# Adding the last four pairs' expert rows to tiles 0 and 1 by 0/1 matrix products

## The chip, the cores and the metric

The kernel runs on one core of one Trainium2 chip. The metric is the device time of one execution in microseconds. TensorE (PE) multiplies matrices, VectorE (DVE) and ScalarE (ACT) work element by element, GpSimd (POOL) does so too and issues indirect transfers, and SyncE (SP) issues the plain transfers. The five engines run their own instruction queues in order and wait for each other by semaphores.

## What is computed

Two layers on 2048 tokens of width 256. The part that matters here is the mixture of experts in the first layer and how its result is used:

```python
topk_w, topk_idx = jax.lax.top_k(scores, K)          # K = 8 of E = 64 experts, CAP = 64 slots each
buf  = zeros.at[dest].set(xf[slot_token])            # gather of tokens to expert slots
hmid = silu(einsum(xb, w_gate)) * einsum(xb, w_up)
yb   = einsum("ecf,efh->ech", hmid, w_down)
out  = zeros((T, h)).at[slot_token].add(yb[dest] * topk_w)   # each token adds up its (at most 8) expert rows
...
x  = x + s * silu(out)                               # s: the first layer's spectral mixing
xn = layernorm(x)                                    # the second layer begins: projections, window attention
```

## The kernel before, in words

Tokens are cut into 16 tiles of 128; four tiles are a sequence. The 64 experts are worked as 32 pairs, 128 slots at a time. The kernel has stages, and each ends with a barrier: an engine reports the end of its part to the semaphore `stage` and waits until all five have.

Stage 3 is the pair loop. For pair j, POOL gathers the 128 token rows (`gather_rows`), TensorE turns them, multiplies by the gate and up weights, turns the product (`expert_turn`) and multiplies by the down weights (`expert_down`); VectorE copies the result to `y0[:, j % 4]`. POOL then scatters it (`scatter_rows`, L2331) to the table `z_d` in HBM. `z_d` was cleared before and has for every tile 8 planes of 128 rows: plane k holds the k-th expert row of each token. The row numbers `put0` are worked out by VectorE at the end of the index chain (L1819 to L1835). `keep_clock` (L971) is a pair of matrix products without use, in each pair. Beside the pairs, "units" of the second layer's weights get their low-rank parts added and are split into two f16 halves; 30 of the 32 pairs or so carry one or two. SP writes the units of `wqk` to HBM in four writes of 1 MB (L783), each when its units are done (`lo_done`).

At the end POOL waits for the landing of all scatters and only then reports the stage's end. Behind the barrier SP reads the 8 planes of tiles 1, 0, 3 and 2, 1 MB each (`load_rows`, L789), then weight group 0 and tables. Tiles 0 and 2 are added up by VectorE in three additions (`summed`, L1895 to L1899), tiles 1 and 3 by TensorE as products with the identity (`rows_summed`, L1054). ScalarE takes a tanh of each sum (`half_gate`, L1457), VectorE makes the new x and its statistics (`finish`, L1905 to L1913), and after two tiles their moments (`spreads`). ScalarE normalises (L1468, L1470), TensorE turns the rows (L1062) and ranks the experts of layer two (L1069), and `project(0)` (L1094) begins the attention. The order of VectorE is written out: summed(0), finish(0), finish(1), spreads, summed(2), finish(3), scales, finish(2), spreads. The rows of tiles 4 to 15 are read in halves later (L792), and POOL adds the second halves by accumulating transfers (L2366, L2371) between its sines (L2354).

## Time and profile before

| | |
|---|---|
| three timed runs | 1118.9, 1122.3, 1123.69 us (median 1122.3) |
| the profiled execution's own time | 1118.6 us |
| its span, first to last instruction | 1116.6 us |
| busy: TensorE, VectorE, ScalarE, POOL | 89%, 76%, 60%, 49% |
| mean granted TensorE clock | 0.955 |

Times in a trace count from the start of the span. The pair loop lies between about 128 and 235 us, and the first projection of the second layer starts at 271.87. A pause of an engine costs time only if the chain that ends last runs through it.

### The profile page before, as it was taken

Reading aid. Unit: us, or ns where it says so; the run is one execution under the profiler, and the core shown is the slowest. Engines: PE = TensorE matmul, PEld = TensorE weight load, DVE = VectorE, ACT = ScalarE, POOL = GpSimd, SP = SyncE. Lnnn points to the kernel's source line nnn. Section 1 sums busy time; section 2 is a strip of 40 time slices with the busy share of each in tenths; the row PEclk is TensorE's granted clock in tenths of the full one; section 3 lists DMA queues with packets and bytes.
Section 4 is the critical chain, followed back from the end, with each engine's and each line's share of the span. In section 5 each row is a group of like instructions: output and inputs, shape, how many; then the busy total and the mean of one; then the engine's idle time right before and its main releaser. Section 6 shows DMA issues by size and latency. Waiting matters only on the chain.

```text
span 1116.6 us, 22230 instructions
## 1 busy us (share of the span) xinstructions
PE 988.5 (89%) x6749; PEld 650.3 (58%) x6749; DVE 851.8 (76%) x2241; ACT 667.4 (60%) x1739; POOL 544.5 (49%) x538
## 2 busy tenths in 40 slices
PE   3967879856999999999999999999988899999985
PEld 2535533334565676666666766767654678885443
DVE  4787548846798779768668899999856887775777
ACT  1733425524768766977866666666646877775332
POOL 0489556621755565544444444544521345553774
PEclk9987989976999999999999999999999999999997
DMA  9979699879562466121211001210049345553443
GB/s 340 338 220 368 161 261 289 287 259 279 81 166 76 115 117 144 36 74 39 63 53 39 32 8 39 91 39 1 1 135 322 98 134 145 147 139 92 133 131 95
DMA packets 97023, 155.99 MB, mean 140 GB/s; under 512 B 12272, under 2 KB 67312, under 8 KB 94096
## 3 DMA queue, kind: packets, MB, share of 16 engines
q1 hardware_dynamic: 77184, 115.42, 31.5%
q0 software_dynamic: 19728, 39.21, 15.8%
q8 instruction: 56, 0.92, 0.3%
q14 instruction: 55, 0.45, 0.1%
HBM read 104.84 MB, written 45.02 MB: 134 GB/s over the span
## 4 chain that ended last, share of the span: by engine, by line
PE 56%; DVE 14%; ACT 9%; issue 6%; DMA 4%; POOL 4%; DVEq 4%; POOLq 1%; ACTq 1%; SPq 0%
PE ps L1094 9%; PE ps L1266 6%; PE ps L1158 5%; PE ps L1146 5%; PE ps L1108 5%; PE ps L1126 3%; PE ps L1212 3%; PE ps L1229 3%; ACT arena L1522 2%; PE ps L1284 2%; PE ps L991 1%; PE ps L1136 1%; PE ps L1008 1%; PE ps L1256 1%; DVE x_sb L1909 1%
## 5 line engine op out<-in xcount | busy, mean ns | idle before, releaser
L2354 POOL TENSOR_TENSOR arena<-arena 128x512 f32<-128x512 f32 x128 | 174.6, 1421 | 98.3 <-ACT arena L1499 98.2
L1094 PE MATMUL ps<-arena 128*128 128x512 f16 x768 | 178.4, 383 | 1.3 <-ACT arena L1499 1.3
L2359 POOL TENSOR_TENSOR arena<-arena 128x512 f32<-128x512 f32 x64 | 67.7, 1057 | 176.0 <-DVE arena L2003 176.0
L2396 POOL DMA_INDIRECT wvo<-xn_d,idx x79 | 75.7, 958 | 113.5 <-PE ps L1256 96.4
L1094 PEld LDWEIGHTS ps<-arena 128*128 128x128 f16 x768 | 75.3, 98 | 93.9 <-ACT arena L1499 3.5
L1522 ACT ACTIVATE arena<-arena 128x128 f32<-128x128 f32 x256 | 99.2, 390 | 38.6 <-DVEq L1998 38.6
L1498 ACT ACTIVATE arena<-ps 64x512 f32<-64x512 f32 x128 | 76.0, 593 | 52.0 <-DVE arena L1971 48.4
L1158 PE MATMUL ps<-wvo,arena 128*128 128x256 f16 x768 | 95.1, 276 | 6.0 <-DVE s_sb L2023 3.2
L1146 PE MATMUL ps<-arena 128*128 128x192 f32 (+1 forms) x512 | 94.5, 328 | 2.4 <-DVE arena L2009 2.4
L1971 DVE TENSOR_TENSOR arena<-ps,wvo 128x512 f32<-128x512 f32 x128 | 84.7, 684 | 15.0 <-PE ps L1094 14.4
L1108 PE MATMUL ps<-wvo,arena 128*128 128x512 f16 x384 | 93.0, 379 | 2.9 <-issue 1.5
L1158 PEld LDWEIGHTS ps<-wvo,arena 128*128 128x128 f16 x768 | 75.4, 99 | 26.0 <-issue 4.3
L1146 PEld LDWEIGHTS ps<-arena 128*128 128x128 f32 x512 | 82.4, 192 | 13.4 <-issue 10.8
L1981 DVE TENSOR_TENSOR arena<-arena 128x512 f32<-128x512 f32 x128 | 85.9, 712 | 3.0 <-POOL arena L2354 3.0
L1266 PE MATMUL ps<-arena,wvo 128*128 x474 | 84.3, 315 | 4.0 <-DVE arena L2200 4.0
L2401 POOL DMA_INDIRECT wvo<-y_d,row x64 | 63.7, 995 | 35.7 <-issue 18.6
L1499 ACT ACTIVATE arena<-ps 64x512 f32<-64x512 f32 x128 | 75.3, 589 | 1.5
L1126 PE MATMUL ps<-arena 128*64 128x128 f32 x1024 | 70.8, 281 | 6.0 <-DVE arena L1981 5.8
L1212 PE MATMUL ps<-arena 128*128 128x512 f16 (+1 forms) x288 | 66.0, 387 | 7.8 <-DVE arena L2189 6.9
L1515 ACT ACTIVATE arena<-ps 128x512 f16<-128x512 f32 x64 | 38.2, 597 | 57.6 <-PE ps L1146 56.9
L1126 PEld LDWEIGHTS ps<-arena 128*64 128x64 f32 x1024 | 55.4, 137 | 16.5 <-issue 15.2
L1995 DVE CUSTOM_DVE_ANT_0 arena<-ps,arena 128x128 f32<-128x128 f32 x256 | 58.6, 284 | 7.0 <-PE ps L1126 6.7
(296 smaller groups left out, 2193.6 us busy)
## 6 DMA issues: line engine op xcount, KB each, us to landing
arena<-wqk_d SPq DMA_DIRECT2D x16, 1024.0 KB, 5.8
arena<-in_wgu SPq DMA_DIRECT2D x32, 384.0 KB, 3.8
y_d<-wvo SPq DMA_DIRECT2D x79, 128.0 KB, 2.4
z_d<-wvo SPq DMA_DIRECT2D x8, 1024.0 KB, 4.3
z_d<-wvo SPq DMA_DIRECT2D x2, 4096.0 KB, 25.6
arena<-in_wdn SPq DMA_DIRECT2D x32, 192.0 KB, 5.3
arena<-z_d SPq DMA_DIRECT2D x12, 512.0 KB, 4.1
arena<-z_d POOLq DMA_DIRECT2D x12, 512.0 KB, 6.7
```

What stands on the lines that cost most here:

```text
L1094: last = pe.matmul(ps[s][:, :], wqk[gg][:, s * DC + c, w, hh * DH:(hh + 1) * DH], hx[bb][:, :, x, c * P:(c + 1) * P], start=(c == 0 and w ...
L1108: last = pe.matmul(values_bank(n, q)[:, :], hx[bb][:, q, x, c * P:(c + 1) * P], wvo16[:, UNITS + c * NG + g, w], start=(c == 0 and w == x) ...
L1126: last = pe.matmul(ps[3][side * WIN:(side + 1) * WIN, q * P:(q + 1) * P], qr[:, u, q * P + side * WIN:q * P + (side + 1) * WIN], kr[:, u, ...
L1146: last = pe.matmul(ps[7][:, k * P:k * P + n], vv[gg][:, k, hh * DH:(hh + 1) * DH], probs[:, k * KW + WIN:k * KW + WIN + n], start=(k == 0) ...
L1158: last = pe.matmul(output_bank(n, half)[:, q % 2 * D:(q % 2 + 1) * D], oT[gg][:, x, hh, q * P:(q + 1) * P], wvo16[:, 2 * g + hh // 2, w, h ...
L1212: last = pe.matmul(ps[2 * (c % 2) + g][0:rows, :], sgw16[:, 2 * d + g, w, c * P:c * P + rows], xb16[:, b % 2, :, x, d * P:(d + 1) * P], st ...
L1266: last = pe.matmul(ps[1 + j % 2][:, 0:2 * F1], xsT[:, j % 4, x, c * P:(c + 1) * P], w13[:, bass.ds(e, 1), w, c * 2 * F1:(c + 1) * 2 * F1]. ...
L1498: nc.scalar.activation(qk_s[0:64, s], ps[s][64:P, :], ACT.Copy)
L1522: nc.scalar.activation(pp[u][:, q], sm[:, q], ACT.Exp, bias=mn[:, q:q + 1], scale=-1.0, accum_out=rs[:, q:q + 1])
L1971: nc.vector.tensor_tensor(qk_c[:, s], ps[s][:, :], cos, ALU.mult).then_inc(cos_rd, 1)
L1981: nc.vector.tensor_tensor(dst, a, b, ALU.add).then_inc(rope_done, 1)
L2354: nc.gpsimd.tensor_tensor(qk_s[:, s], qk_s[:, s], sin, ALU.mult).then_inc(sin_done, 1)
```

## The change

The rows of the last four pairs (28 to 31) that belong to tokens of tiles 0 and 1 are no longer scattered. Their row numbers are raised beyond the table's end, where the scatter's bounds check drops them; the rows of all other tiles are scattered as before. For each of these pairs and each of the two tiles VectorE makes a 128x128 table of zeros and ones early in the pair loop (slot by token: one where the slot holds that token), and TensorE multiplies it with `y0`, which adds the rows into a PSUM bank of the tile. SP reads the planes of tiles 0 and 1 as soon as the scatters of pairs 0 to 27 have landed, inside stage 3, ahead of the last weight write. VectorE adds planes 4 to 7 to planes 0 to 3 (`halved`), and TensorE adds the four that are left into the same PSUM banks. The wait for the scatters' landing moves from POOL, ahead of the barrier, to SP, behind it, ahead of the reads of tiles 3 and 2. Buffers change place so that the early reads find theirs free, and with them the waits of the reads of tiles 4 to 7.

```diff
+        FROM = PAIRS - 4
+        kept_at = {(j, t): R3.take(P, P) for j in range(FROM, PAIRS) for t in range(2) if (j, t) != (PAIRS - 1, 1)}
-        yg_of = [yg[:, 0], yg[:, 1], flat(hx_f[1]...), wqk_f[1]...]
+        yg_of = [wqk_f[1]..., flat(hx_f[1]...), yg[:, 0], yg[:, 1]]
...
-        SUMMED = {0: (mix_done, 1), 2: (mix_done, 2), 1: (table0_mm, 5), 3: (table0_mm, 6)}
+        SUMMED = {0: (table0_mm, 5), 1: (table0_mm, 6), 2: (mix_done, 1), 3: (table0_mm, 7)}
...
-        FIRST_FOUR = (0, 1, 3, 2)
+        FIRST_FOUR = (0, 1, 2, 3)
... SP
+            def put_down(n):
+                for u in range(4):
+                    sp.wait_ge(y0_out[u], 16 * len(range(u, n, 4)))
+            def load_first():
+                put_down(FROM)
+                for t in range(2):
+                    upto(sp, y0_ps, FROM - 1)
+                    load_planes(t)
             for g in range(NG):
+                if g == NG - 1:
+                    load_first()
                 sp.wait_ge(lo_done, 2 * UNITS + 4 * (g + 1))
                 sp.dma_start(wqk_d[g], wqk_parts[:, g]).then_inc(wqk_out, 16)
...
-                    sp.wait_ge(*summed_at(t - TPB))
+                    sp.wait_ge(*summed_at(max(t - TPB, 2 + (t - TPB) // 2)))
...
-            for t in (1, 0, 3, 2):
+            put_down(PAIRS)
+            for t in (3, 2):
                 load_rows(t)
... TensorE
-                keep_clock(6, 2)
+                if j < PAIRS - 1:
+                    keep_clock(6, 2)
...
+            def put_rows(j, t):
+                pe.wait_ge(chosen0, 5)
+                upto(pe, y0_rd, j)
+                pe.matmul(mix_of(t), kept_at[j, t], y0[:, j % 4], start=(j == FROM), stop=False, skip_group_check=True)
...
+                if j >= PAIRS - 2:
+                    for t in range(2):
+                        if j == PAIRS - 2:
+                            put_rows(j - 2, t)
+                        put_rows(j - 1, t)
+            def rows_summed(t):
+                put = t < 2
+                if put:
+                    pe.wait_ge(chosen0, 6 + t)
+                else:
+                    pe.wait_ge(yg_in[t], 16)
+                n = K0 // 2 if put else K0
+                for k in range(n):
+                    last = pe.matmul(mix_of(t), ident[:, :], rows_of(t)[:, k], start=(k == 0 and not put), ...)
+            for t in range(2):
+                put_rows(PAIRS - 1, t)
             stage_end(pe, 3)
...
-            rows_summed(1)
-            rows_summed(3)
+            for t in (0, 1, 3):
+                rows_summed(t)
... VectorE
+            nc.vector.tensor_scalar(rz[:, 0:PAIRS - FROM], tile_no[:, FROM:PAIRS], 2.0, float(NT * K0 * P), ALU.is_lt, ALU.mult)
+            nc.vector.tensor_tensor(row_f[:, FROM:PAIRS], row_f[:, FROM:PAIRS], rz[:, 0:PAIRS - FROM], ALU.add)
+            nc.vector.tensor_copy(rz[:, 0:PAIRS - FROM], idx0[:, FROM:PAIRS])
...
+                if j < 4:
+                    for t in range(2):
+                        nc.vector.tensor_scalar(kept_at[FROM + j, t], iota[:, :], rz[:, j:j + 1], -float(t * P), ALU.subtract, ALU.is_equal)
+                    if j == 3:
+                        dve.drain().then_inc(chosen0, 1)
...
+            def halved(t):
+                a = rows_of(t)
+                dve.wait_ge(yg_in[t], 16)
+                nc.vector.tensor_tensor(a[:, 0:4], a[:, 0:4], a[:, 4:8], ALU.add).then_inc(chosen0, 1)
...
-            summed(0)
+            halved(0)
+            halved(1)
             finish(0)
             finish(1)
             spreads(slice(0, 2))
             summed(2)
+            finish(2)
+            scales(1, slice(0, 2))
             finish(3)
-            scales(1, slice(0, 2))
-            finish(2)
... POOL
-            for u in range(4):
-                pool.wait_ge(y0_out[u], 16 * PAIRS // 4)
             pool.sem_inc(stage, 1)
```

How the instructions stand now is shown at three places. On TensorE at the end of the pair loop, before (L971 is keep_clock, L1000 the turn, L1008 expert_down, L1054 the row sums, a product counted once):

```order
L971 MATMUL ps<-ones_bf 128x512 x2
L1000 MATMUL ps<-ident,arena 96x128
L1008 MATMUL ps<-arena 64x256 x4
L1054 MATMUL ps<-arena,ident 128x256 x16
L1062 MATMUL ps<-ident,arena 128x128 x2
```

and with the change (L1021 is the turn, L1029 expert_down, L1055 the 0/1 products, L1089 the row sums):

```order
L1021 MATMUL ps<-ident,arena 96x128
L1029 MATMUL ps<-arena 64x256 x2
L1055 MATMUL ps<-arena 128x256 x4
L1029 MATMUL ps<-arena 64x256 x2
L1055 MATMUL ps<-arena 128x256 x4
L1089 MATMUL ps<-arena,ident 128x256 x16
L1102 MATMUL ps<-ident,arena 128x128 x2
```

The last keep_clock is gone, four 0/1 products stand between the last two expert_down and four behind them. The number of row sums is the same: four for each of tiles 0 and 1 and eight for tile 3, where it was eight for each of tiles 1 and 3.

On SP from the weight writes on, before (L783 the four weight writes, L789 the planes of tiles 1, 0, 3, 2, L805 group 0):

```order
L783 DMA wqk_d<-arena 128x2048 [waits lo_done] x4
L789 DMA arena<-z_d 128x8x256 [waits stage]
L789 DMA arena<-z_d 128x8x256 x3
L805 DMA arena<-wqk_d 128x2048 [waits wqk_out]
L812 DMA wvo<-in_cos 128x512
```

and with the change (L802 the weight writes, L785 the planes, L824 group 0):

```order
L802 DMA wqk_d<-arena 128x2048 [waits lo_done] x3
L785 DMA arena<-z_d 128x8x256 [waits y0_out3,y0_out2,y0_ps,y0_out1,y0_out0]
L785 DMA arena<-z_d 128x8x256 [waits y0_ps]
L802 DMA wqk_d<-arena 128x2048 [waits lo_done]
L785 DMA arena<-z_d 128x8x256 [waits y0_out2,y0_out1,y0_out3,y0_out0,stage]
L785 DMA arena<-z_d 128x8x256
L824 DMA arena<-wqk_d 128x2048 [waits wqk_out]
```

Two of the four plane reads stand ahead of the last weight write and of the barrier, with waits for scatters of their own.

On VectorE behind the barrier, before (L1895 to L1899 are summed, L1905 to L1913 one finish):

```order
L1895 TENSOR_TENSOR arena<-arena 128x1024 [waits yg_in0,stage]
L1897 TENSOR_TENSOR arena<-arena 128x512
L1899 TENSOR_TENSOR arena<-arena 128x256
L1905 TENSOR_TENSOR arena<-arena,s_sb 128x256 [waits g_ready]
L1907 SCALAR_TENSOR_TENSOR arena<-arena 128x256
```

and with the change (L1939 is halved, L1956 the start of a finish):

```order
L1939 TENSOR_TENSOR arena<-arena 128x1024 [waits yg_in0,stage]
L1939 TENSOR_TENSOR arena<-arena 128x1024 [waits yg_in1]
L1956 TENSOR_TENSOR arena<-ps,s_sb 128x256 [waits g_ready]
L1958 SCALAR_TENSOR_TENSOR arena<-arena 128x256
L1960 TENSOR_TENSOR x_sb<-x_sb,arena 128x256
```

The two small additions of tile 0 are gone, and VectorE now waits for both planes before the first finish, whose input comes from PSUM.

## Rows read from the trace of the kernel before

**Rows 1.** The page: TensorE's busy tenths in 40 equal slices of the span

```profile
PE   3967879856999999999999999999988899999985
```

**Rows 2.** Stretches: length, busy of each engine with its instructions, clock, DMA share, GB/s

```profile
138.00:142.00 4.00, 4.00 (x31) 2.01 (x32) 1.61 (x6) 1.59 (x6) 3.01 (x4) 1.00 1.05 126
...
220.00:230.00 10.00, 10.00 (x70) 4.54 (x70) 8.90 (x20) 5.19 (x14) 3.53 (x5) 1.00 0.81 324
230.00:234.00 4.00, 2.53 (x16) 0.83 (x16) 3.92 (x10) 1.88 (x4) 1.85 (x3) 1.00 0.30 105
...
236.00:238.00 2.00, 0.00 (x0) 0.00 (x0) 0.00 (x0) 0.00 (x0) 0.00 (x0) 0.50 0.98 393
```

**Rows 3.** The chain of waits: start us, us, what

```profile
138.08 12.99 DMA arena<-xn_d,idx
...
234.87 4.04 DMA z_d<-arena,put
...
239.52 8.28 DMA arena<-z_d
```

**Rows 4.** Order in time, 226 to 277: start, us, instructions, idle before

```profile
226.75 0.98 POOL L2331 DMA_INDIRECT z_d<-arena,put  x1 [1.74 <-DVE arena L1879]
...
230.81 0.61 PE L971 MATMUL ps<-ones_bf 128*128 128x512 bf16 x2
...
244.92 5.67 PE L1054 MATMUL ps<-arena,ident 128*128 128x256 f32 x16 [12.39 <-DMA arena<-z_d]
...
250.84 3.72 PE L1054 MATMUL ps<-arena,ident 128*128 128x256 f32 x16 [0.25 <-DMA arena<-z_d]
...
252.79 0.41 DVE L1905 TENSOR_TENSOR arena<-ps,s_sb 128x256 f32<-128x256 f32 x1
...
256.33 1.22 DVE L1895 TENSOR_TENSOR arena<-arena 128x1024 f32<-128x1024 f32 x1
...
258.39 0.43 DVE L1899 TENSOR_TENSOR arena<-arena 128x256 f32<-128x256 f32 x1
...
258.85 0.42 ACT L1457 ACTIVATE arena<-arena 128x256 f32<-128x256 f32 x1 [3.87 <-DVE arena L1899]
...
264.62 0.17 DVE L1924 TENSOR_SCALAR st<-st 128x2 f32<-128x2 f32 x1
...
271.87 4.89 PE L1094 MATMUL ps<-arena 128*128 128x512 f16 x12
```

**Rows 5.** Reads from z_d: L789 all four, its middle two, then L792

```profile
DMA to landing us min/median/max: 5.7/9.5/12.3
...
DMA to landing us min/median/max: 8.3/9.5/10.7
...
DMA to landing us min/median/max: 3.9/4.1/10.2
```

**Rows 6.** Scatters, L2331: the 14 from 200 on, one at 156.8, one at 139.4

```profile
DMA to landing us min/median/max: 2.4/4.3/5.0
...
DMA to landing us min/median/max: 6.7/6.7/6.7
...
DMA to landing us min/median/max: 12.2/12.2/12.2
```

**Rows 7.** Order in time on VectorE, 112 to 137

```profile
112.23 0.68 DVE L680 TENSOR_TENSOR arena<-arena 128x256 f32<-128x256 f32 x1 [3.25 <-ACT arena L1382]
112.84 0.54 DVE L681 TENSOR_TENSOR arena<-arena 128x128 f32<-128x128 f32 x1
...
136.79 0.65 DVE L1864 SCALAR_TENSOR_TENSOR arena<-ps,arena 64x96 f32<-64x96 f32 x2 [0.83 <-ACT arena L1424]
```

**Rows 8.** Order in time on POOL, 260 to 277

```profile
260.18 1.41 POOL L2366 DMA_DIRECT2D arena<-z_d  x1 [24.33 <-DMA arena<-z_d]
...
271.66 1.62 POOL L2366 DMA_DIRECT2D arena<-z_d  x1
...
276.75 1.26 POOL L2354 TENSOR_TENSOR arena<-arena 128x512 f32<-128x512 f32 x1 [3.47 <-ACT arena L1499]
```

More of the change, by code:

```diff
@@ L780, in _, with load_planes @@
                 load_experts(j)
+            def load_planes(t):
+                sp.dma_start(rows_of(t), z_d[t * K0 * P:(t + 1) * K0 * P, :].rearrange("(k p) d -> p k d", p=P)).then_inc(yg_in[t], 16)
+            def put_down(n):
[6 more added lines that the diff above has]
+                    load_planes(t)
             for g in range(NG):
+                if g == NG - 1:
+                    load_first()
                 sp.wait_ge(lo_done, 2 * UNITS + 4 * (g + 1))
@@ L788, in load_rows @@
                 if t < TPB:
-                    sp.dma_start(rows_of(t), z_d[t * K0 * P:(t + 1) * K0 * P, :].rearrange("(k p) d -> p k d", p=P)).then_inc(yg_in[t], 16)
+                    load_planes(t)
                 else:
-                    sp.wait_ge(*summed_at(t - TPB))
+                    sp.wait_ge(*summed_at(max(t - TPB, 2 + (t - TPB) // 2)))
                     sp.dma_start(rows_of(t), z_d[t * K0 * P:t * K0 * P + K0 // 2 * P, :].rearrange("(k p) d -> p k d", p=P)).then_inc(yg_in[t % TPB], 16)
@@ L1046, in _ @@
                     low_rank(n)
-            stage_end(pe, 3)
-            def rows_summed(t):
-                pe.wait_ge(yg_in[t], 16)
-                for k in range(K0):
-                    last = pe.matmul(mix_of(t), ident[:, :], rows_of(t)[:, k], start=(k == 0), stop=(k == K0 - 1))
-                last.then_inc(table0_mm, 1)
+                if j >= PAIRS - 2:
[11 more added lines that the diff above has]
+                for k in range(n):
+                    last = pe.matmul(mix_of(t), ident[:, :], rows_of(t)[:, k], start=(k == 0 and not put), stop=(k == n - 1), skip_group_check=True)
+                last.then_inc(table0_mm, 1)
+            for t in range(2):
+                put_rows(PAIRS - 1, t)
+            stage_end(pe, 3)
             def turn_rows(t, bank):
@@ L1883, in _ @@
                     low_part(n)
-            for n in units_at((PAIRS - 1, "end")):
-                add_low_rank(n)
-                low_part(n - 1)
-                low_part(n)
+                if j < 4:
[3 more added lines that the diff above has]
+                        dve.drain().then_inc(chosen0, 1)
             stage_end(dve, 3)
+            def halved(t):
+                a = rows_of(t)
+                dve.wait_ge(yg_in[t], 16)
+                nc.vector.tensor_tensor(a[:, 0:4], a[:, 0:4], a[:, 4:8], ALU.add).then_inc(chosen0, 1)
             def summed(t):
@@ L1898, in summed @@
                 dve.drain()
-                nc.vector.tensor_tensor(mix[:, u], a[:, 0], a[:, 1], ALU.add).then_inc(mix_done, 1)
+                nc.vector.tensor_tensor(mix[:, 0], a[:, 0], a[:, 1], ALU.add).then_inc(mix_done, 1)
             def finish(t):
```

12 lines of the change are left out of this document (7 added, 5 removed).

## The prediction

> **What bounds the kernel now.** I began with the page's slices: TensorE is busy nine tenths or more in most of them [rows 1], so an edit pays only where TensorE stands still. The stretches around the change [rows 2] and the order in time [rows 4] show such a place: TensorE does nothing for 12.39 us before 244.92, and is granted 0.50 of its clock from 236 on. The chain of waits [rows 3] says why: the last scatter of expert rows (issued 234.87, landed 238.91), the reads of the four token tiles behind it (239.52 to 247.8), VectorE's sums and gates, and only at about 272 the first projection. From there TensorE is busy almost without a gap to the end, so I take what the first projection gains as gained at the end. The order in time then gives the step that ends last for each tile, and the landing times [rows 5, 6] say what a transfer takes, alone and beside others.
>
> Before, the four reads issued at 239.1 to 241.5 land 5.7, 8.3, 10.7 and 12.3 us after their issue [rows 5], that is at 244.8, 247.8, 250.8 and 253.8: 3.0 us per megabyte once they follow each other. Tile 2 has landed at 253.8 but VectorE takes it up only at 256.33, behind the two finishes and the moments of tiles 0 and 1, of which finish(1) and the moments take 3.5 us (252.79 to 256.33) [rows 4]. So VectorE's chain decides: call S the end of the third addition of tile 2 (258.39 + 0.43 = 258.82). From S to the end of the second moments (264.62 + 0.17 = 264.79) are 6.0 us, and 7.1 us more to the first projection at 271.87.
>
> **The reads of tiles 0 and 1.** They now wait for the scatters of pairs 0 to 27 alone. Pair 27's is issued at 226.75 [rows 4]; 4.5 us for its landing (between 4.04 and 5.0, which scatters beside a one megabyte write took, [rows 3, 6]) gives 231.3. SP is free then: its third weight write needs only unit 27, which pair 27 finishes, and the fourth waits for unit 31, four pairs on. With the spacing of [rows 5] the planes land at 231.3 + 5.7 = 237.0 and at 240.0; the scatters of pairs 28 to 31 share the engines with them, at most 4 x 128 KB, about 1.5 us at 350 GB/s if all were moved in that time. Half of that is moved by then, of which I charge 0.4: 240.4.
>
> **The tail of the pair loop.** TensorE's keep_clock pair of pair 31 goes (0.6 us, as the 0.61 us row at 230.81), 16 fp32 instructions of 128x256 come, eight of them ahead of expert_down(31). The same shape took 3.72 us for 16 at full clock, 0.233 us each, and 5.67 us for 16 from half clock upward [rows 4]. Eight are 1.9 us; less 0.6 this moves expert_down(31) by about 1.3 us. VectorE's copy behind it stood in VectorE's queue for some 0.8 us of that, so the scatter starts at about 235.3 in place of 234.87: 0.4 us lost. The other eight end at about 236, beside that scatter's issue, and cost nothing. POOL no longer waits for its landings, so the stage ends at 235.3 + 1.0 = 236.3, before the first plane is there.
>
> **The last scatter and tiles 3 and 2.** The scatter of pair 31 now runs beside the two plane reads and the last weight write. The 14 scatters from 200 on took 2.4 to 5.0 us; the 5.0 is of one issued at 221.4, with the DMA engines at 0.81, the 2.4 of one at 231.9, with them at 0.30. Two early ones took 6.7 and 12.2 us, the latter in a stretch in which the engines were full at 126 GB/s [rows 2, 6]. I take 5.3 us, near the 5.0 us row, since the planes come as whole rows at 350 GB/s as before: it lands at 240.6. The bounds are 4.0 and 12.2. Behind it SP issues tiles 3 and 2. The last weight write (1 MB, 3.0 us behind the planes) ends at 243.4, so tile 3 lands at 246.4 and tile 2 at 249.4. The bytes say the same: 5 MB of reads and writes and 0.4 us of scatters from 231.3 + 2.7.
>
> The Trainium skill (page "DMA: Bandwidth & Descriptors", section on latency and other measured facts) speaks against the edit here: access to HBM takes 0.2 us on average but 2 us at high load, and this makes most of a transfer's fixed cost, so a scatter that was nearly alone gets slower once reads are put beside it. By that figure alone the landing would be 2.4 + 1.8 = 4.2 us, an estimate; the rows show a larger step, 2.4 to 5.0 us. The same page (queues, rings and completion order) has each DMA engine take turns between its queues packet by packet, by which the scatter would not stand behind both planes; the 5.0 us row agrees, the 12.2 us row does not.
>
> **VectorE.** For tiles 0 and 1 it does one addition each of 1.22 us in place of three for tile 0: halved(0) 237.0 to 238.3, halved(1) 240.4 to 241.7. TensorE then adds four planes, 8 instructions, 1.9 us at full clock and 2.8 us at half; tanh takes 0.4. That puts finish(1) at 244.0 to 244.9, and the 3.5 us behind it end at 248.4 at the latest, before 249.4. So what ends last is now the landing of tile 2: S = 249.4 + 2.5 = 251.9, 6.9 us earlier.
> Behind S the order is changed: finish(2), which waits for its tanh (258.85, 0.42 us), now stands ahead of finish(3), whose sum was ready. I charge 0.4 us. The rest of the way to the projection is untouched, 7.1 us, of which 4.89 us for the first 12 matmuls come at half clock [rows 4]; TensorE pauses there as before, so I expect the same clock.
>
> **Edits that should cost nothing, or little.** The three small VectorE instructions added to the index chain (each at most the 0.54 us of the much larger row at 112.84 [rows 7], 1.6 us in all) stand before a 3.25 us wait for ScalarE. The eight comparisons that make the 0/1 tables have the 128x128 shape of that row, so at most 4.3 us in all, 1.1 us in each of pairs 0 to 3, where VectorE waits 0.83 us for the row shown and more for the others. Without that cover they would cost up to 4.3 us; what sticks out of it, and what the index chain may take from POOL, which works beside it, lies between 0 and 1 us: I take 0.1, as pairs 4 on wait for gathers (12.99 us, [rows 3]) anyway. The load of group 0 is issued at about 243.4, when the last weight write has landed, and is there by 253, 12 us before it is needed. Rows of tiles 4 and 5 are asked for at S = 251.9 in place of 250.4 and 250.8, 14 us before the projection in place of 21. POOL's chain there was: a first accumulate at 260.18, a third until 273.28, then a wait of 3.47 us until the first sine at 276.75 [rows 8]. Now tile 4 lands at about 256 (4.1 us after 251.9, [rows 5]), the third issue ends 13.1 us later at 269.1, and the sine is due at 270.5. It is hidden by 1.4 us; I charge 0.1 us for the risk.
>
> **Sum**, against the profiled execution: -6.9 + 0.4 + 0.1 + 0.1 = -6.3 us (the 0.4 us of the later scatter is inside S). That execution took 1118.6 us (its span 1116.6, 2.0 around it); with the change 1112.3. It lies 3.7 us below the median of the three timed runs, 1122.3, so on that scale I forecast 1116.0 us. A measurement of this kernel tells about 0.5%, 5.6 us, from no change: the forecast lies just beyond.
>
> **Rivals.**
> A. The planes slow the last scatters more than the 5.0 us row says. At 6.7 us the scatter lands at 242.0; tile 3 then needs 5.7 us from its issue (247.9) and tile 2 comes at 250.9, S = 253.4: -4.8 us. At 9 us it is -2.5. For it: reads and scatters have never run together at this rate in the trace. Against: 14 scatters beside weight loads and writes took 5.0 at most. Some -3.5 us, 1118.8.
> B. Slower: the same place, but the landing is as between 138 and 146, where a gather took 12.99 us [rows 3] and a scatter 12.2 [rows 6]. The scatter would land at 235.3 + 13.0 = 248.3, tile 2 at 257.0, S = 259.5, 0.7 late, and with the 0.6 of the other edits +1.3 us: 1123.6. It decides from a landing of about 11.8 us on. Against: those engines were full at 126 GB/s, while planes move at 350 (1 MB in 3.0 us).
> C. The gain is given back by POOL: if the accumulates take 2 to 4 us longer because the reads are now packed closer, the first sine and with it the first scores come late, -6.3 + 2.5 = -3.8: 1118.5. For it: only 1.4 us of cover is left. Against: the second wait of POOL (0.78) and VectorE take part of it up.
> D. TensorE pauses less and keeps its clock (2.4 GHz in place of 1.2) until the projection: 4.89 becomes 2.45, 2.4 us more: -8.7, 1113.6. For it: the pause behind the loop shrinks from 12.39 us to about 2. Against: between the row sums and the turned rows it still stands idle for some 5 us, and works in short pieces until the projection.
> E. The change does not do what it says: SP reaches the early reads only at 234, because a scatter of pairs 24 to 27 lands late or the third weight write waits. Planes at 239.7 and 242.7; the fourth write follows and tile 2 comes at 252.1: -3.6, 1118.7.
>
> **How the numbers follow.** Forecast 0.52, A 0.14, B 0.06, C 0.10, D 0.12, E 0.06. The forecast's own range is -4.5 to -8 us. Predicted 1116.0. Over the cases -9.5 to about 0 holds 8 in 10, 1112.8 to 1122.3; the three runs lie up to 3.4 us from their median, of which I add part below and nothing much above: 1110.5 to 1122.5. Faster by over 0.5% needs 5.6 us: D nearly all, three fifths of the forecast and a little for how medians scatter, 0.48. Slower by over 0.5% would need B and more, 0.06. The rest, 0.46, is within.
>
> **What would show it.** The first two z_d reads issued at 231 to 232, landing at 237 and 240; pair 31's scatter issued near 235.3 and landing in 5 to 6 us; TensorE's row sums at 238 and 242; VectorE's first addition of tile 2 waiting for a DMA until about 249.4; 4.89 us at the projection, starting near 265.6; POOL waiting for ScalarE, not for the accumulates, at the first sine. The prediction is wrong if the scatter lands later than 243, if VectorE still comes to tile 2 after it has landed, or if the first projection is early but the end is not.

## The result, and the profile after

The changed kernel takes 1117.34 us (median of 16 runs, 1109.98 to 1120.44), the kernel before 1120.1 us beside it (16 runs, 1116.39 to 1123.69). The ratio is 0.9967, 95% interval [0.9952, 0.9981]: 3.7 us faster, 2.1 to 5.4 (the two medians lie 2.8 us apart). That is a real gain, but inside the 0.5% that I called no change. The profiled execution took 1117.38 us, its span is 1115.2 (before 1118.6 and 1116.6).

The order in time of the changed kernel around the stage's end (start, us, instructions, idle time before):

```profile
224.93 0.98 POOL L2383 DMA_INDIRECT z_d<-arena,put  x1 [1.74 <-DVE arena L1923]
...
229.30 1.01 SPq L785 DMA_DIRECT2D arena<-z_d  x2
229.81 1.99 PE L1055 MATMUL ps<-arena 128*128 128x256 f32 x8
...
232.31 1.99 PE L1055 MATMUL ps<-arena 128*128 128x256 f32 x8
...
233.54 0.34 SPq L802 DMA_DIRECT2D wqk_d<-arena  x1
233.65 0.98 POOL L2383 DMA_INDIRECT z_d<-arena,put  x1 [0.91 <-DVE arena L1923]
...
235.22 1.22 DVE L1939 TENSOR_TENSOR arena<-arena 128x1024 f32<-128x1024 f32 x1 [1.70 <-DMA arena<-z_d]
...
238.70 1.23 DVE L1939 TENSOR_TENSOR arena<-arena 128x1024 f32<-128x1024 f32 x1 [2.26 <-DMA arena<-z_d]
...
240.89 0.99 SPq L785 DMA_DIRECT2D arena<-z_d  x2
...
246.82 5.19 PE L1089 MATMUL ps<-arena,ident 128*128 128x256 f32 x16 [4.85 <-DMA arena<-z_d]
...
249.77 1.23 DVE L1946 TENSOR_TENSOR arena<-arena 128x1024 f32<-128x1024 f32 x1 [3.68 <-DMA arena<-z_d]
...
251.83 0.43 DVE L1950 TENSOR_TENSOR arena<-arena 128x256 f32<-128x256 f32 x1
...
257.35 0.55 DVE L1743 TENSOR_SCALAR st<-st 128x2 f32<-128x2 f32 x1
...
258.75 0.17 DVE L1975 TENSOR_SCALAR st<-st 128x2 f32<-128x2 f32 x1
...
266.00 4.86 PE L1134 MATMUL ps<-arena 128*128 128x512 f16 x12
```

Its chain of waits at the same place (start, us, what), to be held against [rows 3]:

```profile
233.65 7.15 DMA z_d<-arena,put
...
241.31 8.43 DMA arena<-z_d
...
266.11 4.75 PE ps L1134 x12
```

The planes of tiles 0 and 1 are read early and have landed at 235.2 and 238.7. VectorE waits 3.68 us for tile 2's planes, where before it came to them late [rows 4]. The last scatter takes 7.15 us, where it took 4.04 [rows 3].

Absolute times mislead here, since the pair loop itself arrives 1.8 us earlier in this trace (pair 27's scatter at 224.93 against 226.75 [rows 4]). So I measure from that scatter's issue, called P27. (A dash stands where the chain doesn't show the landing.) The table holds distances in us, each the difference of two starts in an order in time: from P27 to pair 31's scatter, to the start of VectorE's second addition of tile 2, and to the first projection; then from one mark to the next: POOL's first and last normalisation in the attention (one for each of 64 heads, L2359 before and L2409 after), the first and ninth gather of the last stage, the span's end. The rows below "other chips" are experiments, told of further down.

| kernel | last scatter | its landing | 2nd addition | projection | to 1st norm. | attention | to 1st gather | to 9th | to end |
|---|---|---|---|---|---|---|---|---|---|
| before | 8.12 | 4.04 | 30.87 | 45.12 | 15.31 | 527.17 | 16.32 | 37.07 | 248.86 |
| changed | 8.72 | 7.15 | 26.14 | 41.07 | 15.28 | 528.60 | 17.41 | 39.07 | 248.84 |
| *other chips* | | | | | | | | | |
| changed_again | 8.64 | 7.22 | 26.17 | 40.73 | 15.57 | 526.83 | 18.93 | 39.55 | 273.57 |
| before_hold | 8.12 | 4.06 | 31.06 | 45.30 | 15.06 | 528.03 | 14.87 | 38.20 | 273.01 |
| after_hold | 8.68 | 7.10 | 26.15 | 40.71 | 15.71 | 527.72 | 14.85 | 36.59 | 272.96 |
| undo_early | 8.63 | 3.99 | 31.45 | 46.02 | 15.06 | 528.23 | 17.42 | 37.50 | 271.04 |
| write_last | 8.72 | 6.02 | 24.86 | 39.40 | 19.55 | 527.49 | 16.22 | 39.66 | 271.92 |
| one_plane | 8.67 | 3.98 | 22.65 | 37.56 | 15.49 | 527.72 | 16.14 | 39.51 | 271.75 |
| write_free | 8.67 | – | 24.71 | 39.25 | 16.31 | 527.74 | 18.93 | 37.73 | 272.60 |
| best | 8.63 | 5.17 | 23.91 | 38.31 | 17.48 | 526.83 | 14.86 | 39.84 | 273.14 |
| best_again | 8.72 | 4.99 | 23.69 | 37.85 | 17.63 | 527.66 | 14.85 | 38.01 | 270.28 |
| entry_hold | 8.72 | 7.12 | 25.82 | 39.76 | 14.94 | 527.89 | 14.86 | 38.01 | 272.26 |
| free_gate | 8.71 | – | 24.99 | 39.54 | 14.89 | 531.54 | 17.42 | 37.14 | 271.53 |
| best_gate | 8.72 | – | 25.94 | 40.48 | 15.96 | 532.43 | 14.86 | 38.39 | 275.20 |

In the first two rows the change gains 45.12 - 41.07 = 4.05 us at the first projection and keeps them to the first normalisation. Behind it the trace of the changed kernel is longer by 1.4 us in the attention, 1.1 on the way to the first gather and 2.0 on the way to the ninth.

### The profile page after: what moved, and what is told of

Read it like the earlier page. It is cut to its first block, busy times and chain, and to the rows that moved or that the text cites. A ratio compares the mean times of both kernels' runs of the same rounds, so it can differ in the third digit from the quotient of the medians.

```text
span 1115.2 us, 22280 instructions
## 1 busy us (share of the span) xinstructions
PE 992.5 (89%) x6763; PEld 652.6 (59%) x6763; DVE 856.1 (77%) x2251; ACT 668.6 (60%) x1739; POOL 544.6 (49%) x538
## 3 DMA queue, kind: packets, MB, share of 16 engines
q0 software_dynamic: 19728, 38.95, 16.1%
## 4 chain that ended last, share of the span: by engine, by line
PE 58%; DVE 14%; ACT 8%; issue 5%; POOL 4%; DMA 4%; DVEq 3%; POOLq 1%; ACTq 1%; SPq 1%
PE ps L1134 9%; PE ps L1306 6%; PE ps L1198 5%; PE ps L1186 5%; PE ps L1148 5%; PE ps L1166 3%; PE ps L1252 3%; PE ps L1269 3%; ACT arena L1562 2%; PE ps L1324 2%; PE ps L926 2%; PE ps L1029 2%; PE ps L1011 2%; PE ps L1176 1%; PE ps L1296 1%
## 5 line engine op out<-in xcount | busy, mean ns | idle before, releaser
L2409 POOL TENSOR_TENSOR arena<-arena 128x512 f32<-128x512 f32 x64 | 67.7, 1058 | 175.8 <-DVE arena L2055 175.8
```

## The experiments

They ran in three series on three other chips, on which the kernel before takes 1152.17, 1152.66 and 1148.13 us (35, 24 and 35 runs), 2.5 to 2.9% more. All ratios are against the kernel before in the same series. No version below is shown to be faster than the changed kernel itself, which stands at 0.9956 in the second series: all their intervals reach that value or lie above it. Theory A: the early reads carry the gain, they slow pair 31's scatter by being beside it, and the rest is given back by TensorE's clock behind the attention. Its rivals: the gain comes from the order of VectorE and the freed barrier; the scatter is slow because of the weight write or the 0/1 products; POOL's accumulates decide.

**Holding the clock at the end of the attention**, with the change and without it.

```diff
                 turn_probs(h)
+                if h == NH - 1:
+                    keep_clock(0, 8)
...
             attend(NH - 1)
+            keep_clock(0, 5)
...
+            upto(pe, xs_lo, 0)
+            keep_clock(4, 10)
             up_proj(0)
```

> The changed kernel with unused 128x512 products at three places where TensorE waits: 8 behind the last turned probabilities, 5 ahead of the last output quarters, 10 ahead of the first up projection of the routed experts. In the changed kernel's trace TensorE's clock is at half from about 816 to 823 and from 850 to 857, before the change only for 2.9 and 2.7 us. Theory 1 (the clock takes the gain back): the half-clock stretches at 816 and 850 are gone or short, and the end comes (6.9 + 7.0)/2 = about 7 us earlier at most, about 5 to 7 us under the changed kernel, near 1111. Theory 2 (transfers of weights or gathered rows of the last stage decide there, the clock is only a bystander): the clock stays up but the end moves by under 1 us.

> The same unused products in the kernel before. Theory 1: its half-clock stretches there are short in the profiled run (2.9 and 2.7 us), so it gains about 1 to 3 us, and the changed kernel with the same products is then faster than this one by about 4.5 us (0.4%), the lead that it has at the end of the attention in the two traces. Theory 2: no gain, and the distance between the two stays as without the products, 0.33% on the median.

Measured: after_hold 1145.17 us (12 runs), ratio 0.9943 [0.9916, 0.997]; before_hold 1149.19 us (12 runs), ratio 0.9988 [0.9952, 1.0024]. The stretches from the last normalisation to the first gather (length, busy time of PE, PEld, DVE, ACT, POOL with instructions, clock, DMA share, GB/s) stand here for five kernels. The kernel before, on the first chip:

```profile
814.40:830.70 16.30, 11.62 (x84) 9.47 (x82) 7.31 (x11) 3.49 (x7) 1.01 (x2) 0.90 0.24 75
```

The changed kernel there:

```profile
809.90:827.30 17.40, 12.72 (x84) 9.98 (x82) 7.29 (x11) 3.51 (x7) 1.02 (x2) 0.80 0.23 71
```

The changed kernel again, on another chip:

```profile
813.50:832.40 18.90, 14.22 (x84) 11.30 (x82) 7.30 (x11) 3.49 (x7) 1.01 (x2) 0.73 0.21 65
```

The changed kernel with the clock held:

```profile
820.90:835.80 14.90, 13.02 (x97) 9.95 (x95) 7.32 (x11) 3.56 (x7) 1.08 (x2) 1.00 0.27 83
```

The kernel before with the clock held:

```profile
824.40:839.30 14.90, 13.02 (x97) 9.92 (x96) 7.30 (x11) 3.56 (x7) 1.05 (x2) 1.00 0.27 84
```

The same 84 products take 11.62, 12.72 or 14.22 us as the granted clock is 0.90, 0.80 or 0.73, and the stretch grows by the same amount. With 13 products without use more it is 14.9 us at clock 1.00, with the change and without: over the table, the six traces with these products show 14.85 to 14.87 and the eight others 16.1 to 18.9. So this loss is the clock's and no wait of the change. Two traces of the same changed kernel differ by 1.5 us here, so how much of it falls on which kernel is chance. The Trainium skill ("TensorE: Matmul & The Clock Gate", part 1) says that the slow clock is the default and activity releases it, and that the number of slow products at one kernel's start varies from run to run; these rows agree, though this stretch lies in the middle of the kernel.

The way from the first to the ninth gather goes with the clock as well: 36.6 us at a granted clock of 1.00 (after_hold), 37.1 to 38.4 in the eight traces at 0.95 or 0.96, 39.1 to 39.8 in the five at 0.91. But here the products don't hold it reliably: best has them and 0.91.

The end did not follow as expected. The changed kernel was to gain 5 to 7 us by the products. after_hold's ratio is 0.13% below that of changed_again, 1.5 us; they ran in different series, and the intervals overlap. before_hold's 1.4 us lies within the noise. What stands is the distance between the two held kernels, 4.0 us on the medians and 5.5 on the means, where 4.5 was expected.

**Reading tiles 0 and 1 behind the barrier again**, with all else as changed.

```diff
             for g in range(NG):
-                if g == NG - 1:
-                    load_first()
...
             put_down(PAIRS)
+            for t in range(2):
+                load_planes(t)
             for t in (3, 2):
                 load_rows(t)
```

> The changed kernel with the reads of tiles 0 and 1 back behind the last scatter's landing (ahead of tiles 3 and 2), all else as changed. Theory A (the early reads carry the gain): the last scatter lands in 4 to 5 us in place of 7.15; the planes land 5.7 to 12.3 us behind it, the first projection comes within 1.5 us of before when counted from pair 27's scatter, and the time is within 0.2% of before. Theory B (the gain is mostly a shorter half-clock stretch at the start of the pair loop, 151 to 154 in place of 150 to 161, and chance): the first projection is still some 2 us earlier than before, with the pair loop earlier by as much, and the time lies between the two kernels.

Measured: 1154.64 us (12 runs), ratio 1.0031 [0.9997, 1.0064]. The chain shows the scatter:

```profile
244.36 3.99 DMA z_d<-arena,put
248.43 5.41 DMA arena<-z_d
```

The projection comes 46.02 us after P27, 0.7 later than in before_hold, the only trace of the old order on these chips. All of the gain at the projection is the early reads'; the 0/1 products, the new order and the freed barrier alone cost a little, as far as one trace of each shows. (The time was to be within 0.2% of before; it is 0.31% above, with an interval from 0.03% below to 0.64% above.) The scatter is back at 3.99 us though the products are there, so these do not slow it.

**What slows the scatter: the last weight write.** The fourth write is moved behind the reads of tiles 3 and 2.

```diff
-            for g in range(NG):
-                if g == NG - 1:
-                    load_first()
-                (wait, write group g)
+            for g in range(NG - 1):
+                keep_group(g)
+            load_first()
...
             for t in (3, 2):
                 load_rows(t)
+            keep_group(NG - 1)
             sp.wait_ge(wqk_out, 16 * NG)
             load_group(0)
```

> The changed kernel with the fourth 1 MB weight write issued behind the reads of tiles 3 and 2, so that pair 31's scatter shares the DMA engines with the two plane reads alone. If the write is half of what slows the scatter (7.15 us from issue to landing, against 4.04 before): landing in 5 to 6 us, tile 2 taken up 1 to 2 us earlier, first projection 1 to 2 us earlier, if VectorE is not the later one. If the planes alone slow it: landing stays near 7 us and nothing moves. Either way group 0 is there 3 us later, unseen.

Measured: 1153.77 us (12 runs), ratio 1.0019 [0.9988, 1.005]. Its chain:

```profile
237.58 6.02 DMA z_d<-arena,put
...
244.73 10.12 DMA wqk_d<-arena
...
257.38 6.16 DMA arena<-z_d
...
264.17 11.14 DMA arena<-z_d
```

and POOL in order of time:

```profile
264.17 1.41 POOL L2419 DMA_DIRECT2D arena<-z_d  x1 [25.60 <-DMA arena<-z_d]
275.60 0.91 POOL L2424 DMA_DIRECT2D arena<-arena  x1 [10.03 <-DMA arena<-z_d]
276.19 1.62 POOL L2419 DMA_DIRECT2D arena<-z_d  x1
276.97 3.35 POOL L2407 TENSOR_TENSOR arena<-arena 128x512 f32<-128x512 f32 x2
```

The scatter takes 6.02 us, 1.1 less (though here the early reads were issued 6.3 us behind P27, 1.9 later than in the changed kernel), and the projection comes 1.3 to 1.7 us earlier than in the changed kernel. But SP's wait for the fourth write holds back the rows of tiles 4 to 7, POOL's first accumulate starts late, and the sine stands behind it without a pause: the first normalisation comes 19.55 us behind the projection. This is rival C's mechanism, brought about by another edit: 1.5 us gained, 4 lost.

**What slows the scatter: the planes.** Of tiles 0 and 1 only plane 0 is read and added, so the early reads are 0.25 MB in place of 2 MB. The rows of the other seven planes are left out of the sums. This was one run without a timed comparison.

```diff
+                n = 1 if t < 2 else K0
-                sp.dma_start(rows_of(t), z_d[t * K0 * P:(t + 1) * K0 * P, :]...)
+                sp.dma_start(rows_of(t)[:, 0:n], z_d[t * K0 * P:(t * K0 + n) * P, :]...)
...
-                n = K0 // 2 if put else K0
+                n = 1 if put else K0
...
-                nc.vector.tensor_tensor(a[:, 0:4], a[:, 0:4], a[:, 4:8], ALU.add).then_inc(chosen0, 1)
+                nc.vector.tensor_tensor(a[:, 0:1], a[:, 0:1], a[:, 0:1], ALU.add).then_inc(chosen0, 1)
```

> The changed kernel with only plane 0 of tiles 0 and 1 read and added (the sums leave out 7 planes of each). The weight write stays. If the 2 MB of planes are what slows pair 31's scatter: it lands in about 4 to 4.5 us in place of 7.1 and tile 2 is taken up about 2.5 to 3 us earlier, unless VectorE's own work is later. If it is the write (1 us less in write_last) or the wait for what a slower scatter queue has before it: over 6 us.

```profile
242.10 3.98 DMA z_d<-arena,put
246.60 8.16 DMA arena<-z_d
```

3.98 us with the weight write in place, as before the change. So it takes the planes to slow the scatter: with them and the write it is 7.1 to 7.2 (changed, changed_again, after_hold, entry_hold). With the planes alone it is 6.02 in write_last, but there the early reads were issued late. In two traces of the best version, told of below, they were issued 4.4 us behind P27 as in the changed kernel, and the write comes only after the scatter has landed (best, then best_again):

```profile
245.37 5.17 DMA z_d<-arena,put
234.84 4.99 DMA z_d<-arena,put
```

Like for like the planes alone therefore cost 1.0 to 1.2 us, and the write beside them 2.0 to 2.2 more; from write_last it would be 2.0 and 1.1. The write costs this only in company. The projection at 37.56 is about what the change would give if the planes were free, 7.7 us over before_hold; VectorE and TensorE also have less to add there.

Why the early reads come late in some traces can be seen at the semaphore of pair 27's scatter, for which SP waits. In each of the eleven traces with early reads 15 of its 16 parts land by 4.2 to 4.3 us. The last one lands with them in six; in after_hold, best_gate, write_free, write_last and free_gate it lands at 5.2 to 6.1, and the reads are issued at 5.3 to 6.3. The edits leave this wait alone, so it counts as chance here. It takes up to 1.9 us of the head start.

**The changed kernel again**, beside the next versions.

> The changed kernel once more, beside the others of this series, as their common base. From the first series: pair 31's scatter lands in 7.1 us and the first projection starts 41 us behind pair 27's scatter (41.07 and 40.71 seen, 45.1 and 45.3 before the change). Theory 1 (the clock decides how much of it arrives): this distance repeats within 0.5 us, while the stretches between the last normalisation of the attention and the first gather of the last stage (17.41 in the first trace), and the one from there to the ninth gather (39.07), differ from trace to trace with the half-clock stretches in them. Theory 2: those two repeat as well.

Measured: 1147.48 us (12 runs), ratio 0.9956 [0.9928, 0.9984]. Projection 40.73, scatter 7.22 us: the local numbers repeat on another chip, 4.6 us before before_hold's and 3.9 to 4.1 at the first normalisation (56.30 in changed_again, 56.42 in after_hold, 60.36 in before_hold).

**The write moved without its wait.** Group 0 is loaded after three writes have landed, and the fourth goes last.

```diff
-            keep_group(NG - 1)
-            sp.wait_ge(wqk_out, 16 * NG)
+            sp.wait_ge(wqk_out, 16 * (NG - 1))
             load_group(0)
+            keep_group(NG - 1)
```

> As write_last, but group 0's load waits for the first three weight writes alone and goes ahead of the fourth, so that SP does not stand 10 us before the reads of tiles 4 to 7. If the loss of write_last from the first projection to the first normalisation (19.55 us against 15.3) is SP's wait for the fourth write: that distance returns to 15.1 to 15.7 us, pair 31's scatter still lands in 6.0 us, the first projection comes 39 to 40 us behind pair 27's scatter, and the time is 1 to 2 us under the changed kernel. If it is the number of transfers beside the accumulates: the distance stays over 17 us.

Measured: 1147.18 us (12 runs), ratio 0.9951 [0.9924, 0.9978]. Projection 39.25 as in write_last; 16.31 us from there to the first normalisation, so the loss is mostly, but not wholly, cured (15.1 to 15.7 was expected). In sum 55.56 against 56.30 us. The time was to be 1 to 2 us below the changed kernel's and is not: the means of the two are the same, 1146.85. The chain doesn't show the scatter's landing, but the last packet on its queue ends 5.3 us behind its issue, which in the other traces is 0.35 to 0.5 us ahead of the landing: 5.6 to 5.8 us.

**The best version.** write_free, with the clock held at the end of the attention and ahead of the projection.

```diff
-            for t in (0, 1, 3):
-                rows_summed(t)
+            for t, n in ((0, 5), (1, 20), (3, 16)):
+                rows_summed(t)
+                keep_clock(5, n)
...
+                    if t == 2:
+                        keep_clock(5, 8)
```

> write_free with unused 128x512 products in TensorE's waits: those of after_hold, and 5, 20 and 16 of them behind the row sums of tiles 0, 1 and 3, 8 ahead of the turned rows of tile 2. Theory 1 (clock): the half clock between about 246 and 270 goes or shrinks, the first 12 products of the first projection take about 2.6 us in place of 4.9, the first projection comes 1 to 2 us earlier still, and the end 5 to 9 us before the changed kernel on the same chip. Rival: the unused products stand in front of the turned rows and delay them by as much as they give back; then no more than write_free.

> The best version so far once more, for a comparison in the same series: ratio to the kernel before 0.990 to 0.996, the first projection 38.3 us after pair 27's scatter, the first normalisation 17.5 us later. If the version with the later accumulates is worth its 1.6 to 2.4 us, it stands 0.14 to 0.21% below this one.

Measured: 1143.23 us (7 runs), ratio 0.9932 [0.9904, 0.9961], and in the next series 1143.41 us (12 runs), 0.9959 [0.9931, 0.9986]. It beats the kernel before in both. Over the changed kernel it has the lower ratio in the first, but the intervals overlap, so that it beats this one too isn't shown; 5 to 9 us below it were expected, and the means lie 2.7 apart. In the first 4.9 us of the projection the clock is 0.66 in best, with 16 products done, and 1.00 in best_again, with 23 (the changed kernel: 0.56, 14). So the added products don't always hold it there. The projection comes at 38.31 and 37.85, and 17.5 us later the first normalisation. POOL again:

```profile
269.91 1.41 POOL L2427 DMA_DIRECT2D arena<-z_d  x1 [23.56 <-DMA arena<-z_d]
280.32 0.91 POOL L2432 DMA_DIRECT2D arena<-arena  x1 [9.00 <-DMA arena<-z_d]
280.91 1.62 POOL L2427 DMA_DIRECT2D arena<-z_d  x1
281.69 3.35 POOL L2415 TENSOR_TENSOR arena<-arena 128x512 f32<-128x512 f32 x2
```

The accumulate takes 9 us and more from its issue, the projection is now 5.3 us ahead of its end, and the sine behind it no longer waits for ScalarE. What was gained at the projection ends in this wait: to the first normalisation it is 55.8 and 55.5 us, as in write_free.

**The clock held, the write in its place** (the two holds on the changed kernel).

> The changed kernel with the clock held ahead of the projection and at the end of the attention, the weight write in its own place. Pair 31's scatter lands after 7.1 us as in the changed kernel. If holding the clock ahead of the projection is worth what it was in the best version beside the moved write (38.3 against 39.3 us, 0.9 us), the projection comes 39.8 us after pair 27's scatter in place of 40.7, and the first normalisation 15.1 to 15.7 us later. If the held clock only fills pauses that end with a transfer, it stays at 40.7. With the hold at the end of the attention the ratio to the kernel before is 0.992 to 0.996.

Measured: 1144.21 us (12 runs), ratio 0.9962 [0.9934, 0.9989]. The projection comes at 39.76 as expected, 1.0 us earlier than in changed_again, and 14.94 us later the first normalisation: 54.7 us, the shortest of all but one_plane (53.1) and free_gate (54.4). Holding the clock ahead of the projection is worth 1.0 us in this trace, where the moved write gave 1.3 to 1.5, and here the first normalisation doesn't come later for it. The whole time shows nothing of it: 0.9962 here, 0.9956 for the changed kernel.

**Fewer accumulates ahead of the sines.** The tanh of tiles 4 to 7 and with them their accumulates come one head later.

```diff
-        GATE_AT = {4: 0, 5: 1, 6: 2, 7: 3, 8: 6, ...}
+        GATE_AT = {4: 1, 5: 2, 6: 3, 7: 4, 8: 6, ...}
```

> The version with the last weight write behind the load of group 0, without any held clock, and the tanh of tiles 4 to 7 with their accumulates one head later. Theory (the accumulates' issues stand ahead of POOL's first sine): the first normalisation comes 15.1 to 15.7 us after the first projection in place of 16.3, and the projection stays 39.3 us after pair 27's scatter; about 0.6 to 1.2 us. Rival: the 16.3 us are another wait and stay.

> As the best version so far (planes of tiles 0 and 1 early, last 1 MB weight write behind the load of group 0, clock held ahead of the projection and at the end of the attention), and the tanh of tiles 4 to 7 with their accumulates on POOL one head later. In the best version the first projection came 38.3 us after pair 27's scatter, but the first normalisation 17.5 us after the projection, where it is 15.1 to 15.7 with the write in its old place; on POOL the third accumulate is issued at 280.91 and ends at 282.5, and the first sine stands behind it. Theory: the sine waits for that accumulate's issue, which waits for the first accumulate's landing. With only one accumulate ahead of the sines the first normalisation comes 15.1 to 15.9 us after the projection, 1.6 to 2.4 us of gain kept to the end of the attention: ratio to the kernel before 0.990 to 0.993. Rival: VectorE and TensorE are late for another reason (the clock, the order of their work); then 17 to 17.5 us stay. Second rival: the accumulates come late for the tanh of tile 4 or 5, and head 1 to 5 grow: attention from first to last normalisation above 528.5 us.

Measured: free_gate (on write_free) 1148.53 us (12 runs), ratio 0.9989 [0.9958, 1.002]; best_gate (on the best version) 1143.89 us (12 runs), 0.9973 [0.9942, 1.0004]. In free_gate POOL waits for ScalarE again at the first sine:

```profile
268.39 1.41 POOL L2419 DMA_DIRECT2D arena<-z_d  x1 [22.56 <-DMA arena<-z_d]
280.57 2.52 POOL L2407 TENSOR_TENSOR arena<-arena 128x512 f32<-128x512 f32 x2 [10.77 <-ACT arena L1542]
```

and the first normalisation comes 14.89 us after the projection in place of 16.31. So the queue on POOL was the cause, as the theory had it. But the attention grows from 527.74 to 531.54 us, all of it by head 7: the starts of the eighth normalisation lie 61.78 us behind the first where they lay 57.98. The second rival holds too, and at 3.8 us costs more than the 1.4 gained. best_gate says the same of the attention (532.43 against 527.66); its projection comes 2.2 us later than the best version's. There the early reads were issued 1.2 us later (the late part of pair 27's scatter), the row sums of tile 0 took 3.75 us in place of 1.97, and VectorE came to tile 2 at 24.65 us from P27, 1.6 behind its landing, where in best it waited for it. Which engine is late in heads 3 to 7 wasn't followed up.

## Why the prediction was right, and where it was not

It forecast 1116.0 us and a gain of 6.3. The time came out at 1117.34 and the gain at 3.7. That the time is only 1.3 us off is partly luck: the forecast started from 1122.3, the median of three runs, and over 16 runs the kernel before takes 1120.1. The gain itself lies below the 4.5 to 8 us given for it, though its interval reaches to 5.4. Faster by over 0.5%, held a little likelier than no change (0.48 against 0.46), did not come. By steps:

- *The early reads.* Forecast: issued at 231.3, landed 237.0 and 240.4. From P27 that is 4.5, 10.2 and 13.6 us; measured 4.4 (229.30), 10.3 (235.22) and 13.8 (238.70). Right.
- *The tail of the pair loop.* Pair 31's scatter was to be 0.4 us later; it is 0.6 (8.72 against 8.12 from P27). The eight 0/1 matmuls took 1.99 us, forecast 1.9.
- *The last scatter.* This is the term that was mis-sized: "I take 5.3 us, near the 5.0 us row". It took 7.15, and 7.1 to 7.2 in every repeat. S, forecast 25.15 us after P27 (251.9 - 226.75), came at 27.33 (252.26 - 224.93): of the 2.2 us missing 1.85 are the scatter's landing, 0.2 its later issue and 0.2 the reads behind it. The gain at S is 32.07 - 27.33 = 4.7, where 6.9 was forecast. This is rival A's mechanism. By its own prices (4.8 us of net gain left at a landing of 6.7 us, 2.5 at 9) 7.15 leaves 4.35; the projection came 4.05 us earlier. The experiments put 1.0 to 2.0 us on the planes and the rest, 1.1 to 2.2, on the write beside them.
- *The reading behind that term.* "14 scatters beside weight loads and writes took 5.0 at most" is wrong. The view gives the least, middle and greatest of the landings that it knows, and of these 14 it knows three: 4.27 (issued at 209.02), 4.99 (221.38) and 2.43 (231.87). The packets of the queue, 32 of 4 KB for each scatter, show the others. The one issued at 215.93, beside two weight writes of 1 MB issued at 215.53 and 216.57, has its last packet 7.75 us behind its issue, and the next one, at 219.01, 5.82. In the changed kernel the landing of that same pair is known. It was issued at 214.09, beside the writes at 213.68 and 214.72 and 15 us ahead of the early reads (line L2383, window 213.5 to 215):

```profile
DMA to landing us min/median/max: 8.1/8.1/8.1
```

So the trace of the kernel before already held a scatter slowed more than pair 31's would be, with no read of `z_d` beside it. The upper price was in it.
- *The rule that was weighed.* The Trainium skill ("DMA: Bandwidth & Descriptors", latency and other measured facts, 0.2 us on average and 2 us at high load) gives +1.8 us on a transfer's fixed cost, an estimate. The steps by the planes alone, 1.0 to 2.0 us over 3.98, have that size. The 8.1 us beside two writes does not, and no run separates a slower access from waiting behind the other transfers' bytes. In the three traces without the write whose landings are known (best, best_again, write_last) the scatter lands within 0.6 us of the second plane read, which was issued 2.0 to 3.9 us ahead of it.
- *What ends last.* VectorE now waits for tile 2's planes, and finish(0), finish(1) and the moments end at 246.1, before them. Right.
- *Behind S.* From S to the end of the second moments it was to be 0.4 us longer, and is 0.7 (258.92 - 252.26 = 6.66 against 5.97); 0.3 in changed_again. The rest is one small instruction, 0.55 us at 257.35 in place of 0.16 in changed_again, where POOL issues a transfer beside it as well; a chance, as far as the traces show. From there to the projection 7.08 us, as before, with 4.86 us for the first 12 matmuls: the clock stayed at half, rival D did not come.
- *POOL's cover.* The wait of 3.47 us at the first sine [rows 8] was to shrink to 1.4; it is 1.26. Right, and on this chip the way from the projection to the first normalisation is as long as before. On the others it goes with the clock: 15.06 us at 0.88 and 0.89 (before_hold, undo_early), 15.57 at 0.84 (changed_again), 15.71 at 0.83 (after_hold). Rival C did not come; it needs the first accumulate later or longer, which only the moved write brought.
- *"What the first projection gains is gained at the end."* The local gain is 4.05 us. The profiled execution is only 1.2 us shorter, although its pair loop had arrived 1.8 us early: 1.4 us were lost in the attention, 1.1 between it and the first gather, and 2.0 from there to the ninth. The clock has a large part in the last two; the first is in the experiments, the second is seen in these stretches (columns as above). The kernel before:

```profile
855.00:860.00 5.00, 5.00 (x36) 3.58 (x36) 2.92 (x5) 2.94 (x7) 0.00 (x0) 0.85 1.08 318
```

The changed kernel:

```profile
851.60:856.60 5.00, 5.00 (x22) 2.87 (x23) 2.91 (x4) 1.94 (x4) 0.00 (x0) 0.50 1.10 282
```

TensorE does 36 products in 5 us at clock 0.85 and 22 at 0.50. In the table the way from the first to the ninth gather, in which these 5 us lie, takes between 36.6 and 39.8 us, on either side of both. In the attention 0.8 us of the 1.4 fall at heads 15 and 16, which changed_again does not show (heads 1 to 14 take the same time to 0.03 us in both and before); its attention is 526.83 us, shorter than before's. So most of the loss there is not the change's. One part is: the step at head 21 is 0.34 to 0.36 us longer in all twelve traces with the new instruction order than in the two with the old one. In the changed kernel VectorE stands still for 0.44 us there, ahead of L1964, and the profile names nothing that it waits for; the cause is open. Over many runs these chances average out: the ratio's 3.7 us is close to the local 4.05.

So the mechanism was right, one term was 1.85 us too small because rows were read as covering scatters that they don't, and the profiled execution alone would have said that two thirds of the gain get lost, which its repeats do not bear out.

What stays open: the steps in the attention, and why the other chips are slower with the same instructions. The pair loop reaches P27 at 226 to 237 us on them, but most of the difference lies in the last column of the table, 270 to 275 us where the first chip takes 249. The half-clock stretches of the pair loop lie at other places from trace to trace, but I didn't tie them to it one by one.

## What to carry to other kernels

A transfer that ends a stage is not free to share its time with the ones it was meant to overlap: price it by the nearest row that runs beside as many bytes, and where there is none take the upper bound, not the middle. Look how many transfers such a row covers: a view of landings leaves out those that it doesn't know. Measure a local gain from a mark just ahead of the change, since the granted clock moves everything behind it by 1 to 4 us from trace to trace; and when a gain ends at a queue with slow issues in it (POOL's accumulates here), the next microsecond needs that queue cut as well, with a look at who waits for what was moved.

## What the runs showed of the hardware

- An indirect scatter of 128 rows lands after 4.0 us beside one 1 MB write (before, undo_early, one_plane), 5.0 to 6.0 beside 2 MB of plain reads from the same table (best, best_again, write_last), 7.1 to 7.2 beside both (four traces), and 8.1 beside two 1 MB writes and the pair loop's weight loads, with no read of the table (changed, issued at 214.09). Pair 31's scatter leaves out the rows of tiles 0 and 1 in all of these but before.
- Of the 16 parts in which such a scatter lands, one can be 0.9 to 1.9 us behind the 15 others (pair 27's in five traces of eleven with early reads), and a wait for the whole scatter takes that long.
- The first accumulating transfer of 512 KB from HBM holds POOL back for 9 to 10 us from the end of its issue (rows with 9.00 and 10.03 of waiting), beside other reads; a later one, issued at 268.01 in the changed kernel, lands 7.4 us behind its issue. The plain reads of 512 KB take 4.1 in the middle [rows 5].
- Products without use, put where TensorE paused, held clock 1.00 through the end of the attention in six traces of six. Between the first and the ninth gather they did not: best has 0.91 there.
